# Attention and gated FFN in one fp32-exact kernel: values as one wide product a token tile, and the order at the seams

## The chip, the cores and the metric

One core of one Trainium2 chip. The metric is the device time of one execution in microseconds (us), the median of several. Engines: PE (TensorE, matmul), PEld (its weight loads), DVE (VectorE), ACT (ScalarE), POOL (GpSimd), SP (SyncE, which here only issues DMAs).

## The reference

`x` is 8 sequences of 1024 tokens with 512 features, fp32.

```
xn = layernorm(x)
heads: ql,kl,vl = xn @ local_qkv      full softmax attention
       qs,ks,vs = xn @ sparse_qkv     scores below the 102nd largest of a row masked, softmax
       xp = xn @ memory_proj; softmax(xp @ bank.T) @ bank; concat @ mem_out + b
       (xn @ pred_in + b) @ pred1 + b -> gelu -> @ pred2 + b
s = concat(4 heads of 128) @ warboss_w + b          # 512 x 512
g = silu(relu(xn @ w1 + b1) @ w2 + b2)              # 512 -> 2048 -> 512
out = x + s * g
```

## The kernel before

Every product is exact to fp32: each operand is split in a high part (rounded to fp32r, a reduced form of fp32 that PE takes) and a low part (the rest), and `product` (L72 to L76) issues three matmuls, high by high, high by low, low by high. So nearly every result of PE is read twice or more: a copy of the high part (a rounding copy by ACT) and a subtraction for the low part (by DVE or POOL).

**Stage 1** works over 16 halves of a sequence, 512 tokens each. It makes queries, keys, values and the memory and prediction heads, and writes them in split form to scratch arrays in DRAM. What PE does in a half is a list of jobs in the order of `JOBS` (L49; half 0 has `FIRST_JOBS`). mp and pi project for memory and prediction, ql, qs, kl, ks are queries and keys, ms the memory scores, p1a and p1b the first prediction layer (before gelu), wt the transposed memory weights, p2 the second layer, tr0 to tr3 transpose the next half's normalised tokens, mo is the memory output, v01 and v23 are the values of token tiles 0, 1 and 2, 3 (both value heads, 256 columns a tile). The jobs take six PSUM banks in turn: `PLACE` numbers them, `bank` is the place modulo 6, and a job waits until the bank of the job six places before it has been read (`bank_free`, semaphore `bank_read`, counted by ACT's last copy of each job). Where DVE reads the bank after ACT (mp, pi, wt) the next user waits for `lo_ready` too (`LOW_OF`).

All engines walk the same list. ACT (`scalar`, L564 on) copies each job out, does the gelu of p1a and p1b (L586, to SBUF) and of the values makes one copy (L620) and one rounded copy (L622). POOL (`gpsimd`, `left` L514 to L516) subtracts for the low parts of queries, keys, values and the FFN weights. DVE (`vector`, L798 on) makes the other low parts (`subtract`, L673), in gelu's case a rounding cast (L858) and a subtraction, and the softmax of the memory head. It also makes the layer norm of half n + 2 at the end of half n (`layer_norm_parts`, L675 to L715): statistics (L693, L696), then twelve steps of Newton's method for the inverse root on 128 x 4 elements (L699 to L707), then the application (L711). Halves 2 to 5 also split a quarter of the warboss weights there. Half 14 starts the search for the first slot on `early`, `scores` and `ranks`: ACT copies the scores (L649), DVE takes maxima (L766 on).

**Stage 2** works over 64 slots of 128 tokens. A slot has one row of scores for each attention head, PE's transposes of the probabilities, the outputs, the mixing product `mix`, and four chunks of the FFN: `f1` (hidden, `hid` or `o` from `xnT` and `w1`) and `f2` (`acc` from `w2` and `h`). DVE finds the 102nd largest score by rounds of MAX8 and MATCH_REPLACE8 over two half rows (L1561 to L1584), and between the rounds, at the round numbers `R_MAX` and `R_INVERSE`, takes the full row's maximum (`full_max`, L1529) and the inverse of its sum (`full_inverse`, L1535). The order of `f1`, `f2`, `transposes`, `head_scores` and `head_out` on PE is written out in `slot` (L1725 on; the last slot behind it). SP's DMA queue loads `w1`, `w2`, `tl` and the keys and values, in the order written in its `slot` (L1239 on). C is the number of a chunk, c its number within the sequence.

## Time and profile before

| | us |
|---|---|
| median of 3 runs | 2529.58 (2529.27 to 2530.76) |
| profiled execution | 2529.44, its span 2527.6 |
| PE busy | 2515.6 |
| DVE busy | 2291.1 |
| ACT busy | 1299.4 |
| POOL busy | 1151.8 |

The span runs from the first to the last instruction. Times of instructions are counted from the start of the span, so a row that starts at 246.78 lies in stage 1 (to about 485), one at 565.03 in slot 3 of stage 2. One half of stage 1 takes 29.14 us, one slot 31.83. The clock granted to TensorE was 1.00 of full speed throughout, the higher of its two levels.

### The profile page before, as it was taken

The numbers are of one execution on the slowest core, as the hardware profiler recorded it, in microseconds if no ns is written. First come the engines' busy times: TensorE is split into PE (matmuls) and PEld (weight loads), VectorE is DVE, ScalarE is ACT, GpSimd is POOL, SyncE is SP. The second block draws the span as 40 slices with busy tenths as digits, with TensorE's granted clock in tenths as the row PEclk, the third lists the DMA queues.
The fourth block names the chain that finished last, engine by engine and source line by source line (L and its number), as shares of the span: only waits on it lengthen the run. The fifth ranks groups of instructions, "written<-read, shape, count | busy, mean of one in ns | idle before, by whom it ended". The sixth has DMA issues, their size and how long they took to land.

```text
span 2527.6 us, 36088 instructions
## 1 busy us (share of the span) xinstructions
PE 2515.6 (100%) x12432; PEld 2120.0 (84%) x12432; DVE 2291.1 (91%) x5184; ACT 1299.4 (51%) x2128; POOL 1151.8 (46%) x975
## 2 busy tenths in 40 slices
PE   9999999999999999999999999999999999999999
PEld 8888888878888888888888888888888888888887
DVE  7566556999999999999999999999999999999995
ACT  5666666644444444444544444444444444444443
POOL 2544444533444444444444444444444444444444
PEclk9999999999999999999999999999999999999999
DMA  8888888964655565546554665466556654665443
GB/s 262 331 309 314 309 311 326 340 230 138 236 197 200 167 234 200 200 167 233 200 200 166 224 206 197 166 219 214 200 167 216 215 199 164 216 217 199 165 157 122
DMA packets 166149, 551.74 MB, mean 218 GB/s; under 512 B 17936, under 2 KB 32976, under 8 KB 157648
## 3 DMA queue, kind: packets, MB, share of 16 engines
q1 hardware_dynamic: 165680, 548.90, 61.9%
q8 instruction: 101, 1.65, 0.3%
q14 instruction: 80, 0.66, 0.1%
q10 hardware_dynamic: 288, 0.52, 0.1%
HBM read 415.15 MB, written 134.22 MB: 217 GB/s over the span
## 4 chain that ended last, share of the span: by engine, by line
PE 95%; DVE 4%; ACT 0%; issue 0%; POOL 0%; POOLq 0%; ACTq 0%
PE acc L74 9%; PE acc L76 9%; PE acc L75 9%; PE hid L76 9%; PE hid L74 9%; PE hid L75 9%; PE ps L74 5%; PE ps L76 5%; PE ps L75 5%; PE o L1709 4%; PE scores L1696 4%; PE o L1713 2%; PE scores L74 2%; PE scores L76 2%; PE scores L75 2%; PE o L75 2%
## 5 line engine op out<-in xcount | busy, mean ns | idle before, releaser
L1428 POOL TENSOR_TENSOR h_lo<-h,h_hi 128x512 fp32r<-128x512 f32 x254 | 336.0, 1323 | 719.7 <-ACT h_hi L1323 718.2
L1561 DVE MAX8 ranks<-early 128x8 f32<-128x512 f32 x819 | 564.7, 689 | 13.0
L1581 DVE MATCH_REPLACE8 early<-ranks,early 128x512 f32<-128x512 f32 x756 | 511.1, 676 | 0.0
L1322 ACT ACTIVATE h<-hid,small 128x512 f32<-128x512 f32 x255 | 175.7, 689 | 479.9 <-PE hid L76 479.8
L74 PE MATMUL acc<-w,h_hi 128*128 128x512 f32 x1016 | 408.0, 402 | 0.0
L76 PE MATMUL hid<-xnT,w 128*128 128x512 f32 x1020 | 397.5, 390 | 0.0
L74 PE MATMUL hid<-xnT,w 128*128 128x512 f32 x1020 | 397.0, 389 | 0.0
L75 PE MATMUL hid<-xnT,w 128*128 128x512 f32 x1020 | 396.8, 389 | 0.0
L76 PE MATMUL acc<-w,h_lo 128*128 128x512 f32 x1016 | 396.5, 390 | 0.0
L75 PE MATMUL acc<-w,h_hi 128*128 128x512 f32 x1016 | 396.5, 390 | 0.0
L1428 POOL TENSOR_TENSOR pT_s<-pT,pT_s 128x512 fp32r<-128x512 f32 x256 | 327.2, 1300 | 42.2 <-ACT pT_s L1337 42.2
L1565 DVE MAX8 ranks<-early 128x8 f32<-128x512 f32 x441 | 298.2, 676 | 0.0
L1584 DVE MATCH_REPLACE8 early<-ranks,early 128x512 f32<-128x512 f32 x378 | 255.6, 676 | 0.0
L76 PEld LDWEIGHTS acc<-w,h_lo 128*128 128x128 f32 x1016 | 190.7, 188 | 41.4
L74 PEld LDWEIGHTS hid<-xnT,w 128*128 128x128 f32 x1020 | 191.5, 188 | 40.3 <-DMA w<-ffn_scratch 0.4
L76 PEld LDWEIGHTS hid<-xnT,w 128*128 128x128 f32 x1020 | 191.5, 188 | 39.8
L75 PEld LDWEIGHTS hid<-xnT,w 128*128 128x128 f32 x1020 | 191.5, 188 | 39.6
L75 PEld LDWEIGHTS acc<-w,h_hi 128*128 128x128 f32 x1016 | 191.6, 189 | 33.6
L74 PEld LDWEIGHTS acc<-w,h_hi 128*128 128x128 f32 x1016 | 191.3, 188 | 33.7
L516 POOL TENSOR_TENSOR tiles_out<-tiles_out 128x512 fp32r<-128x512 f32 x64 | 95.1, 1495 | 227.3 <-ACT tiles_out L609 226.5
L1323 ACT ACTIVATE h_hi<-hid,small 128x512 fp32r<-128x512 f32 x253 | 172.6, 682 | 0.0
L1457 POOL TENSOR_TENSOR gate<-gate,mixed 128x512 f32<-128x512 f32 x60 | 77.8, 1297 | 186.1 <-DVE gate L1514 186.1
(237 smaller groups left out, 5170.2 us busy)
## 6 DMA issues: line engine op xcount, KB each, us to landing
w<-ffn_scratch SPq DMA_DIRECT2D x512, 512.0 KB, 4.1
xnT_scratch<-xnT SPq DMA_DIRECT2D x16, 2048.0 KB, 13.7
kv_scratch<-kv_out SPq DMA_DIRECT2D x32, 1024.0 KB, 6.1
tl<-tile_scratch SPq DMA_DIRECT2D x64, 512.0 KB, 4.0
tile_scratch<-tiles_out SPq DMA_DIRECT2D x15, 2048.0 KB, 8.5
xnT<-xnT_scratch SPq DMA_DIRECT2D x60, 512.0 KB, 7.1
ffn_scratch<-ffn SPq DMA_DIRECT2D x16, 1024.0 KB, 4.3
values<-kv_scratch SPq DMA_DIRECT2D x16, 1024.0 KB, 6.2
```

Source lines behind the costliest of these rows:

```text
L74: nc.tensor.matmul(out, w_hi, x_hi, start=first, stop=False)
L75: nc.tensor.matmul(out, w_hi, x_lo, start=False, stop=False)
L76: return nc.tensor.matmul(out, w_lo, x_hi, start=False, stop=last)
L1322: nc.scalar.activation(h32[:, c % 2, :], src[:, :], ACT.Relu, bias=bias)
L1323: nc.scalar.activation(h_of(C, c)[0], src[:, :], ACT.Relu, bias=bias).then_inc(h_h, 1)
L1428: return nc.gpsimd.tensor_tensor(out_, value, hi_.bitcast(F32), ALU.subtract).then_inc(ready, 1)
L1561: l_step = count(nc.vector.max(top_l[:, own], larger[:, :]))
L1565: s_step = count(nc.vector.max(top_s[:, own_s], smaller[:, :]))
L1581: l_step = count(nc.vector.match_replace(larger[:, :], top_l[:, own], larger[:, :], LOWEST))
L1584: s_step = count(nc.vector.match_replace(smaller[:, :], top_s[:, own_s], smaller[:, :], LOWEST))
L1696: last = nc.tensor.transpose(scores[:, j * P:(j + 1) * P], prob[own][:, j * P:(j + 1) * P], ident[:, :])
L1709: nc.tensor.matmul(o[:, :], units[unit][:, u, HI, c], pT_s[:, j, :, :, :], start=j == 0, stop=False)
```

## The change

1. The values are four jobs, v0 to v3, one a token tile. The high and low parts of the projection weights lie side by side in `wp_s`; a tile's high part is multiplied by both in one product of 512 columns (four of them, one for each quarter of the features), then its low part by the high weights in four of 256 columns. The three partial products then stand in two sums. ACT copies both to the two places of `kv_out` in one operation; POOL adds them, rounds the sum and subtracts, with a semaphore (`v_step`) between the steps.
2. Gelu: ACT applies it in place in PSUM, then makes the rounded copy; DVE subtracts each bank by itself, and its cast is gone. p1a and p1b are in `LOW_OF`.
3. The banks are shifted by four, since a half now has 20 jobs.
4. The layer norm of half 2, which DVE made whole at the end of half 0, is divided: statistics at the end of half 0, Newton's steps behind mp of half 1, the application behind pi.
5. At the seam of the stages: f1(0) and f1(1) wait for other banks; in slot 1 the two f2 stand before head_scores and before the second transposes, in slot 2 the f2 of chunk C stands before the wait for the transposes; in slot 3 the maximum of the full row and its inverse come one round earlier; SP issues w2(2) before tl(2) and w1(4) early.
6. In the last slot three f2 stand each one place earlier.

```diff
 JOBS = ["mp", "pi", "ql", "ms", "p1a", "p1b", "qs", "kl", "wt", "ks", "p2",
-        "tr0", "tr1", "tr2", "tr3", "mo", "v01", "v23"]
-FIRST_JOBS = ["mp", "pi", "ql", "ms", "p1a", "p1b", "qs", "kl", "ks", "v01", "wt", "tr0", "p2", "tr1", "mo", "tr2",
-              "tr3", "v23"]
+        "tr0", "tr1", "tr2", "tr3", "mo", "v0", "v1", "v2", "v3"]
+VALUES = ["v0", "v1", "v2", "v3"]
+FIRST_JOBS = ["mp", "pi", "ql", "ms", "p1a", "p1b", "qs", "kl", "ks", "v0", "v1", "wt", "tr0", "p2", "tr1", "mo",
+              "tr2", "tr3", "v2", "v3"]
 BANKS = 6
+BANK_SHIFT = 4
...
-    LOW_OF = {"mp": "xp", "pi": "pin", "wt": "wt"}
+    LO = ["xp", "pin", "first_gelu", "gelu", "wt"]
+    LOW_OF = {"mp": "xp", "pi": "pin", "p1a": "first_gelu", "p1b": "gelu", "wt": "wt"}
...
-        wp_hi = sb("wp_hi", [P, KT, 8 * P], F32R)
-        wp_lo = sb("wp_lo", [P, KT, 8 * P], F32R)
+        wp_s = sb("wp_s", [P, 2, KT, 8 * P], F32R)
+        wp_hi, wp_lo = wp_s[:, HI, :, :], wp_s[:, LOW, :, :]
...
-            return PLACE[n, name] % BANKS
+            return (PLACE[n, name] + BANK_SHIFT) % BANKS
...
-                        elif name in ("v01", "v23"):
-                            c = slice(2 * P * slot, 2 * P * (slot + 1))
-                            left(kv_out[:, 2:4, LOW, c], kv_out[:, 2:4, HI, c], kv_l)
+                        elif name in VALUES:
+                            c = slice(P * slot, P * (slot + 1))
+                            high, low = kv_out[:, 2:4, HI, c], kv_out[:, 2:4, LOW, c]
+                            done_steps = 2 * (HTILES * n + slot)
+                            nc.gpsimd.tensor_tensor(low.bitcast(F32), high.bitcast(F32), low.bitcast(F32), ALU.add)\
+                                .then_inc(v_step, 1)
+                            pool.wait_ge(v_step, done_steps + 1)
+                            nc.gpsimd.tensor_copy(high, low.bitcast(F32)).then_inc(v_step, 1)
+                            pool.wait_ge(v_step, done_steps + 2)
+                            left(low, high, kv_l)
                         else:
...
-                            last = nc.scalar.activation(gelu[:, c, :], src, ACT.Gelu, bias=b_p1[:, c:c + 1])
+                            nc.scalar.activation(src, src, ACT.Gelu, bias=b_p1[:, c:c + 1]).then_inc(gelu_step, 1)
+                            act.wait_ge(gelu_step, 2 * n + c + 1)
+                            last = nc.scalar.activation(gelu_hi[:, c, :], src, ACT.Copy)
...
-                        elif name in ("v01", "v23"):
-                            c = slice(2 * P * int(name == "v23"), 2 * P * int(name == "v23") + 2 * P)
-                            src = src.rearrange("p (t h n) -> p t h n", t=2, h=2)
-                            nc.scalar.activation(kv_out[:, 2:4, LOW, c].bitcast(F32)
-                                                 .rearrange("p h (t n) -> p t h n", n=P), src, ACT.Copy)
-                            last = nc.scalar.activation(kv_out[:, 2:4, HI, c]
-                                                        .rearrange("p h (t n) -> p t h n", n=P), src, ACT.Copy)
+                        elif name in VALUES:
+
+                            c = slice(P * int(name[1]), P * int(name[1]) + P)
+                            last = nc.scalar.activation(kv_out[:, 2:4, :, c].bitcast(F32),
+                                                        src.rearrange("p (s h n) -> p h s n", s=2, h=2), ACT.Copy)
...
+                    if n == 1:
+                        next(second)
                     if first(n):
                         dve.wait_ge(bkT_out, 1)
                         subtract(bkT_s[:, 1, :, :], bkT[:, :, :], bkT_s[:, 0, :, :]).then_inc(bkT_split, 1)
...
                                                    op0=ALU.add, op1=ALU.subtract).then_inc(lo_ready, 1)
                     if first(n):
                         low_weights(VL, 2)
+                    if n == 1:
+                        next(second, None)
                     if n in parts:
                         next(parts[n])
...
-                    dve.wait_ge(bank_read, done(n, "p1b"))
-                    nc.vector.tensor_copy(gelu_hi[:, :, :], gelu[:, :, :]).then_inc(ghi_ready, 1)
-                    dve.wait_ge(ghi_ready, n + 1)
-                    subtract(gelu_lo[:, :, :], gelu[:, :, :], gelu_hi[:, :, :]).then_inc(lo_ready, 1)
+                    for c, name in enumerate(("p1a", "p1b")):
+                        dve.wait_ge(bank_read, done(n, name))
+                        subtract(gelu_lo[:, c, :], ps[:, bank(n, name), :], gelu_hi[:, c, :]).then_inc(lo_ready, 1)
...
                         nc.vector.tensor_scalar(half_bias[:, :], half_bias[:, :], 0.5, None, ALU.mult)
-                    if n < LAST - 1:
+                    if first(n):
+                        next(second)
+                    elif n < LAST - 1:
...
-                        elif name in ("v01", "v23"):
+                        elif name in VALUES:
                             v = slice(VL * P, (VS + 1) * P)
                             if first(n):
                                 pe.wait_ge(w_split, 5)
-                            for tt in range(2):
-                                t = 2 * int(name == "v23") + tt
-                                c = slice(t * P, (t + 1) * P)
-                                for k in range(KT):
-                                    last = product(nc, dst[:, tt * 2 * P:(tt + 1) * 2 * P], xnT[:, hh, k, HI, c],
-                                                   xnT[:, hh, k, LOW, c], wp_hi[:, k, v], wp_lo[:, k, v],
-                                                   k == 0, k == KT - 1)
+                            c = slice(P * int(name[1]), P * int(name[1]) + P)
+                            for k in range(KT):
+                                nc.tensor.matmul(dst, xnT[:, hh, k, HI, c], wp_s[:, :, k, v], start=k == 0, stop=False)
+                            for k in range(KT):
+                                last = nc.tensor.matmul(dst[:, 0:2 * P], xnT[:, hh, k, LOW, c], wp_hi[:, k, v],
+                                                        start=False, stop=k == KT - 1)
...
+        FIRST_ROUNDS = {1: (1, 2), 3: (2, 3)}
...
-                sp.wait_ge(f1_done, C - W1_RING + 1)
+                sp.wait_ge(f1_done, 1 if C == 4 else C - W1_RING + 1)
...
+                    load_w2(2, 2)
                     load_tl(2, 2, 2)
-                    load_w2(2, 2)
+                    load_w1(4, 4)
                     load_w2(3, 3)
...
-                load_w1(C + 4, c + 4)
+                if m > 1:
+                    load_w1(C + 4, c + 4)
...
-                r_max, r_inverse = (1, 2) if m == 1 else (R_MAX[T % HTILES], R_INVERSE[T % HTILES])
+                r_max, r_inverse = FIRST_ROUNDS.get(m, (R_MAX[T % HTILES], R_INVERSE[T % HTILES]))
...
                 if C == 0:
-                    pe.wait_ge(shared.bank_read, PLACE[LAST, "wt"] + 1)
+                    pe.wait_ge(shared.bank_read, PLACE[LAST, "p2"] + 1)
                     pe.wait_ge(shared.w10_first, 16)
                     pe.wait_ge(shared.xnT_first, 16)
                 elif C == 1:
-                    pe.wait_ge(shared.bank_read, PLACE[LAST, "ks"] + 1)
+                    pe.wait_ge(shared.bank_read, PLACE[LAST, "mo"] + 1)
...
+                    if m == 2:
+                        f2(C, c, h)
                     pe.wait_ge(pT_h, 4 * g + 2)
                     pe.wait_ge(ps_ready, m)
                     transposes(2)
-                    f2(C, c, h)
+                    if m > 2:
+                        f2(C, c, h)
                     f1(C + 2, c + 2, h)
...
+                    if m == 1:
+                        f2(C, c, h)
                     pe.wait_ge(pT_h, 4 * g + 2)
                     head_scores(T % TL_RING, T_QL, U_KL, sl_done)
-                    f2(C, c, h)
+                    if m > 1:
+                        f2(C, c, h)
                     if not known_first(m, 2):
 
                         pe.wait_ge(mix_ready, m - 2)
                         mix(m - 2, (T - 2) % TL_RING)
                     f1(C + 2, c + 2, h)
+                    if m == 1:
+                        f2(C + 1, c + 1, h)
 
                     pe.wait_ge(pl_ready, m + 1)
                     transposes(0)
-                    f2(C + 1, c + 1, h)
+                    if m > 1:
+                        f2(C + 1, c + 1, h)
                     f1(C + 3, c + 3, h)
...
             f2(C, c, h, (0,))
             f1(C + 2, c + 2, h)
+            f2(C + 1, c + 1, h, (0,))
             pe.wait_ge(mix_ready, m - 2)
             head_out(g, U_VS)
             f1(C + 3, c + 3, h)
-            f2(C + 1, c + 1, h, (0,))
+            f2(C + 2, c + 2, h, (0,))
             pe.wait_ge(at_l, g + 1)
             mix(m - 2, (m - 2) % TL_RING)
-            for i in (2, 3):
-                f2(C + i, c + i, h, (0,))
+            f2(C + 3, c + 3, h, (0,))
             pe.wait_ge(mix_ready, m - 1)
```

On POOL, a half of stage 1 from the third on. Before, `kv_out` 128x2x256 are the low parts of the values:

```order
L516 TENSOR_TENSOR ffn<-ffn 128x2x512
L516 TENSOR_TENSOR kv_out<-kv_out 128x512 x2
L516 TENSOR_TENSOR tiles_out<-tiles_out 128x4x128 x2
L516 TENSOR_TENSOR kv_out<-kv_out 128x2x256 x2
L516 TENSOR_TENSOR tiles_out<-tiles_out 128x4x128 x2
```

With the change:

```order
L519 TENSOR_TENSOR ffn<-ffn 128x2x512
L519 TENSOR_TENSOR kv_out<-kv_out 128x512 x2
L519 TENSOR_TENSOR tiles_out<-tiles_out 128x4x128 x2
L535 TENSOR_TENSOR kv_out<-kv_out 128x2x128
L538 CAST kv_out<-kv_out 128x2x128
L519 TENSOR_TENSOR kv_out<-kv_out 128x2x128
```

The last three rows stand there four times, once for each of v0 to v3, where two operations stood.

On ACT, from the table load ahead of gelu. Before:

```order
L586 ACT_TABLE_LOAD
L586 ACTIVATE gelu<-ps,small 128x512 x2
L608 ACTIVATE tiles_out<-ps 128x4x128
L609 ACTIVATE tiles_out<-ps 128x4x128
L615 ACTIVATE kv_out<-ps 128x512
```

With the change:

```order
L596 ACT_TABLE_LOAD
L596 ACTIVATE ps<-ps,small 128x512
L598 ACTIVATE gelu_hi<-ps 128x512
L596 ACTIVATE ps<-ps,small 128x512
L598 ACTIVATE gelu_hi<-ps 128x512
L620 ACTIVATE tiles_out<-ps 128x4x128
```

Two copies now stand ahead of the copies of qs (`tiles_out`) and of all behind it.

On PE in slot 1, where `scores<-kl` is head_scores and `acc<-w2_0` is f2(0). Before:

```order
L74 MATMUL scores<-kl,tl1 128x512
L75 MATMUL scores<-kl,tl1 128x512
L76 MATMUL scores<-kl,tl1 128x512
L74 MATMUL acc<-w2_0,h_hi 128x512
L75 MATMUL acc<-w2_0,h_hi 128x512
L76 MATMUL acc<-w2_0,h_lo 128x512
```

With the change:

```order
L76 MATMUL acc<-w2_0,h_hi 128x512
L77 MATMUL acc<-w2_0,h_hi 128x512
L78 MATMUL acc<-w2_0,h_lo 128x512
L76 MATMUL scores<-kl,tl1 128x512
L77 MATMUL scores<-kl,tl1 128x512
L78 MATMUL scores<-kl,tl1 128x512
```

The twelve products of f2(0) moved ahead of the six of head_scores.

## Rows read from the trace of the kernel before

**Rows 1.** The page: busy time by engine, and the search's removal operation.

```profile
PE 2515.6 (100%) x12432; PEld 2120.0 (84%) x12432; DVE 2291.1 (91%) x5184; ACT 1299.4 (51%) x2128; POOL 1151.8 (46%) x975
...
L1581 DVE MATCH_REPLACE8 early<-ranks,early 128x512 f32<-128x512 f32 x756 | 511.1, 676 | 0.0
```

**Rows 2.** Windows: us; busy PE, PEld, DVE, ACT, POOL; PEclk, DMA share, GB/s.

```profile
161.10:190.24 29.14, 29.14 (x167) 25.46 (x166) 18.25 (x44) 19.19 (x38) 13.34 (x9) 1.00 0.82 307
493.90:565.00 71.10, 68.31 (x323) 56.17 (x321) 69.97 (x160) 32.97 (x51) 24.31 (x22) 1.00 0.71 254
```

**Rows 3.** Waits of PE: total us, times, longest.

```profile
PE scores L1696 <- ACT early L1372: 2.0, 1, 2.0
...
PE scores L1696 <- ACT pT_s L1337: 0.9, 1, 0.9
PE scores L74 <- ACT pT_s L1337: 0.7, 1, 0.7
...
PE o L1709 <- POOL pT_s L1428: 0.4, 1, 0.4
```

**Rows 4.** Timeline of PE, half 4: first and last of two runs of products.

```profile
134.10 0.39 PE L76 MATMUL ps<-xnT,wp_lo 128*128 128x512 f32 x1
...
139.54 0.39 PE L76 MATMUL ps<-xnT,wp_lo 128*128 128x512 f32 x1
...
154.97 0.28 PE L74 MATMUL ps<-wp_hi,xnT 128*128 128x256 f32 x1
...
160.60 0.28 PE L76 MATMUL ps<-wp_hi,xnT 128*128 128x256 f32 x1
```

**Rows 5.** Timelines of ACT, DVE and PE in half 0.

```profile
31.59 1.27 ACT L586 ACTIVATE gelu<-ps,small 128x512 f32<-128x512 f32 x2
...
38.22 0.69 DVE L673 TENSOR_TENSOR act_hi<-ps,act_hi 64x512 fp32r<-64x512 f32 x1 [1.35 <-ACT act_hi L577]
...
39.02 0.47 PE L74 MATMUL ps<-act_hi,sm_hi 128*128 128x512 f32 x1
```

**Rows 6.** Timeline of ACT, half 7.

```profile
239.69 0.69 ACT L605 ACTIVATE tiles_out<-ps,small 128x512 f32<-128x512 f32 x1 [0.27 <-PE ps L76]
```

**Rows 7.** Timelines of ACT, DVE and PE in half 14.

```profile
439.76 1.05 ACT L649 ACTIVATE early<-scores 128x1024 f32<-128x1024 f32 x1
...
440.83 1.77 DVE L766 TENSOR_TENSOR early<-early 128x512 f32<-128x512 f32 x1
...
446.67 0.48 PE L74 MATMUL ps<-act_hi,sm_hi 128*128 128x512 f32 x1
```

**Rows 8.** Timelines of POOL and PE in the last slot.

```profile
2508.79 1.30 POOL L1428 TENSOR_TENSOR xnT<-h,xnT 128x512 fp32r<-128x512 f32 x1
...
2510.15 0.49 PE L74 MATMUL acc<-w,xnT 128*128 128x512 f32 x1
```

**Rows 9.** Timelines of POOL, DVE and PE, end of half 7, start of half 8.

```profile
246.63 1.30 POOL L516 TENSOR_TENSOR kv_out<-kv_out 128x512 fp32r<-128x512 f32 x1 [1.19 <-ACT kv_out L622]
...
246.78 1.16 DVE L699 TENSOR_SCALAR small<-small 128x4 f32<-128x4 f32 x1
...
253.07 0.68 DVE L673 TENSOR_TENSOR act_lo<-ps,act_hi 128x512 fp32r<-128x512 f32 x1
...
256.33 0.22 PE L987 MATMUL ps<-bkT_s,act_hi 128*128 128x128 f32 x1
```

**Rows 10.** DVE's groups by line in stage 1: busy us, mean ns, idle before.

```profile
L705 DVE TENSOR_TENSOR small<-small 128x4 f32<-128x4 f32 x48 | 21.7, 452 | 1.6
...
L699 DVE TENSOR_SCALAR small<-small 128x4 f32<-128x4 f32 x16 | 15.1, 941 | 0.5
...
L701 DVE TENSOR_SCALAR small<-small 128x4 int32<-128x4 int32 x16 | 2.7, 172 | 0.6
```

**Rows 11.** Timeline of POOL in stage 2: operations of 256 columns.

```profile
507.93 0.74 POOL L1446 TENSOR_TENSOR pT<-pT 128x256 f32<-128x256 f32 x1 [0.80 <-ACT pT L1345]
508.73 0.40 POOL L1448 CAST at_hi<-pT 128x256 fp32r<-128x256 f32 x1
```

21 lines of the change are left out of this document (11 added, 10 removed).

## The prediction

> **What bounds the kernel now.** The page comes first. TensorE (PE) is busy for 2515.6 of 2527.6 us, VectorE (DVE) for 2291.1, ScalarE (ACT) for 1299.4, GpSimd (POOL) for 1151.8 [rows 1]. So the time is PE's own work plus some 12 us in which it stands. Next the table by stretches: in one half of stage 1, 161.10 to 190.24, PE is busy for 29.14 of 29.14 us at a granted clock of 1.00, while ACT works 19.19, DVE 18.25 and POOL 13.34 [rows 2]. PE is the only bound there, and the others have 10 us or more of room in sum, though not always where they need it. Then PE's waits: outside the start only a few are left, 2.0, 0.9 and 0.7 us at the border of the stages, for results of ACT, and 0.4 at the end [rows 3]. A change can win in two ways: fewer us of PE work, or those waits; it loses wherever something that PE waits for comes later than PE does.
>
> I count from the profiled execution, 2529.44 us. It is 0.14 below the median of the runs, 2529.58, so I add 0.14 at the end. What a measurement can tell from no change is about 0.2%, 5.1 us.
>
> **Values on PE.** In half 4 the last 48 products of 256 columns run from 154.97 to 160.60, 47 steps of 0.120 us. The products of 512 columns before them run from 134.10 to 139.54 in 24 steps of 0.2267 [rows 4]. A token tile had 12 of the narrow ones; it gets 4 wide and 4 narrow. Two narrow ones, 0.240, become one wide one, 0.2267: 0.0133 less, 16 times a half, 16 halves: **-3.4 us**. Read as a fixed cost and a cost by columns, both prices give 13 ns a product. The Trainium skill ("TensorE: Matmul & The Clock Gate", section "Wait — 56ns, not 53.3ns?") gives some 2.5 ns above the columns for each matmul in a warm stream; by it the 256 products fewer would bring only 0.6 us. Our rows show four to five times that, and the sum goes by them; if nothing at all were fixed, the gain would be 0, which is the upper end.
>
> **Gelu and startup.** ACT gets two copies a half (0.68 us each, by the neighbours in [rows 5]) and waits between gelu and copy; DVE's cast and its long subtraction become two subtractions of 512 from PSUM. In half 0 ACT is the bottleneck: after the gelus (1.27 for two, at 31.59) it works without a gap, then the DVE subtraction act_hi starts at 38.22 when ACT's act_hi has ended, 1.35 us after DVE was free, and PE's mo starts at 39.02 [rows 5]. The two copies, overlapped with their neighbours as ACT's operations are (starts 0.5 apart for durations of 0.6), and two short waits make some 1.2 us, all of it on this path: **+1.2**. Ends: 0.8 (a wait of PE before p2 of some 0.3 to 0.4 goes, because gelu_lo no longer is one long operation) to 1.6.
>
> **Half 1** gets the third layer norm's small operations before and between mp and pi. They come while POOL still works on half 0, whose values are now 12 operations. I take **+0.3**, ends 0 and 0.9 (one POOL operation of 0.74 each time for one of them).
>
> **The halves after.** Each has ACT 1.3 later from the gelus on. ACT itself waits 0.27 for PE at p2 before [rows 6], and its later results are wanted 0.3 to 0.7 after they come, as I read from their neighbours. So ACT may come some 0.3 late without cost, and its copies absorb the rest before tr0. I take **0**, ends 0 and +0.2 a half (2.4 over twelve).
>
> **Half 14**, where the first slot's search begins, has no room. ACT copies the scores at 439.76, DVE's first maximum follows at 440.83, and behind DVE's two passes over `early` act_hi and PE's mo come at 446.67 [rows 7]. That copy stands behind the gelus, so the whole chain moves by the two copies, 1.36, less the wait that PE shows now (0.15): +1.2, and with the waits **+1.4**; ends 0 (ACT's order lets DVE's subtractions catch up, since they save 0.5) and 1.8.
>
> **The border.** Waits of 0.7, 0.9 and 2.0 us are what can go [rows 3]. In slot 1 f2(C) now runs before head_scores and fills the first. But from 493.90 to 565.00 DVE is busy for 69.97 of 71.10 us [rows 2]: it is the bound behind the other two. head_scores starts 12 products of 0.2267, 2.7 us, later, less the wait of 0.7: the maximum that DVE takes of it comes 2.0 later, and everything behind it. Against that full_max moves one round forward in slot 3, and a round, two MAX8 and two MATCH_REPLACE8 of 676 ns each [rows 1], slightly overlapped, is 2.5 us. The two nearly cancel: 2.0 - 2.5 = -0.5 at slot 3's wait. I take **-0.3**, as w2(1), which f2(C+1) now wants 2.7 us earlier, may come a little late; ends -3.6 (all three go) and +1.0. On SP's queue w2(2) now passes tl(2), and w1(4) passes w2(3); neither is wanted within 4 us of its landing, so nothing.
>
> **The last slot.** The wait of 0.4 goes [rows 3], but POOL's h_lo, from 2508.79 to 2510.09, releases the next f2 at 2510.15 in both orders [rows 8]. **0**, ends 0 and -0.6.
>
> **Sum:** -3.4 + 1.2 + 0.3 + 0 + 1.4 - 0.3 + 0 = **-0.8**. 2529.44 - 0.8 + 0.14 = **2528.8 us**.
>
> **Rival B: POOL's twelve short operations block the layer norm, slower.** DVE's Newton steps are tiny operations that wait for POOL. In the half shown L699 starts at 246.78 and lasts 1.16, ending with POOL's 1.30 from 246.63 [rows 9]. Over stage 1 L699 takes 941 ns on average and L705 452, L701 of the same size 172 [rows 10]: a POOL operation under way blocks the DVE operation until its end. The Trainium skill ("SBUF — State Buffer", section "Who interferes with whom") says the same of a DVE operation that needs the port pair shared with GpSimd: who issues first keeps it for the whole instruction and the other fully blocks. The trace agrees: 941 against 172 ns. After the change POOL has, by the same forms in stage 2 (0.74, 0.40, and 0.73 for the subtraction) [rows 11], some 1.9 us for each of four value jobs, nearly without a gap, from about 246 to 254.4: over the whole Newton chain. If each of its 12 small operations gets in only between two of POOL's, the chain lasts 12 x 0.62 = 7.5 us instead of 4.5, from 247.5 (the subtraction of p1a and p1b and the mixing weights leave it 0.7 later) to about 254.9. The four applications and mp's low part (1.83 and 0.68, as now up to 253.75) end at 257.4. PE wants it at 256.33 [rows 9], 0.2 earlier with shorter values: up to 1.3 us a half; I take 0.85, as POOL's work is over by then and the last operations run free. Halves 1 to 13: 13 x 0.85 = 11. **2540 us.** It decides from the point where the chain gets longer by more than 1.7 us (2.4 of room, 0.7 used up by the later start). For it: 941 against 172 ns, in the half shown just while POOL was at work. Against: POOL waits for its own semaphores between its steps, and in each gap a DVE operation of 0.16 us may slip in, two or three one after the other; then 6 waits of 0.55 make 3.3, hardly over the room, and it costs next to nothing.
>
> **Rival C: the waits go and the new work hides, faster.** The startup and half 14 take less than I say because the DVE operations there no longer meet POOL (1.2 and 1.4 are then 0 to 0.4), and of the border's 3.6 us some 3 go: -3.4 - 3.0 - 0.6 = -7.0. **2522.6 us.** For it: each wait of [rows 3] is at a place which the change touches. Against: DVE nearly without a gap in [rows 2].
>
> **Rival D: ACT is late in every half.** If the 1.3 us of copies outrun ACT's room by 0.2 in twelve halves: 2528.8 + 2.4 = **2531.2**, not told from no change.
>
> **Rival E: the wide products do not save.** If the cadence is set by columns alone: 2528.8 + 3.4 = **2532.2**, also within 0.2%.
>
> **Chances.** My sum has 0.27, D 0.05, E 0.05: 0.37 for within 0.2% (2524.5 to 2534.6). B has 0.36, with mild forms of it counted in: slower. C has 0.27. The range leaves out the tails of B and C: from 2521 (C with a little more) to 2542 (B at 1 us a half). The likeliest case's own range is 2526 to 2533.
>
> **What would show it.** PE should show 12176 matmuls, 256 fewer, and about 2512 us of busy time with steps of 0.227 in the wide products. ACT's busy time should rise by some 22 us (32 copies of 0.68), DVE's fall by some 9 (32 of 0.68 in place of 16 of 0.68 and 16 of 1.2 or more, less what POOL blocks), POOL's rise by 16 x 5 = 80 (7.5 for 2.6). PE's waits should name act_hi in half 0 and in half 14 at about 1.3 each, and none in halves 2 to 13. B is right if PE waits for act_lo or for DVE's mp part at every ms, and L701 to L707 rise from 0.17 towards 0.6 us. C is right if the waits behind ACT at slots 1, 2 and 3 are gone. My forecast falls if PE stands anywhere in halves 2 to 13 for more than 0.3 us a half, or if the step of the wide products is not 0.227.

## The result, and the profile after

The changed kernel takes 2535.76 us (median of 13 runs, 2535.03 to 2536.47), the kernel before 2530.76 (13 runs, 2529.27 to 2531.46) in the same comparison: a ratio of 1.0021, 95% interval 1.0014 to 1.0028. It is slower by 5.0 us, 0.2%. The forecast was 2528.8 and no change; 2535.76 lies inside its range, but the kernel moved, and not by any one of the cases as they were told. The profiled execution took 2535.20, its span is 2533.4 against 2527.6. Executions of the kernel before come out near 2529.4 or near 2531.1 (e11 suggests why), so below, differences of medians under 1 us say little, and the profiles, one for each kernel, say more.

The page's busy times [rows 1]:

```profile
PE 2515.0 (99%) x12176; PEld 2105.5 (83%) x12176; DVE 2299.6 (91%) x5184; ACT 1316.4 (52%) x2160; POOL 1218.3 (48%) x1135
```

PE issues 256 matmuls less, and still the kernel is longer: PE stands more often. The signs of the forecast for the other engines were off too: ACT's busy time rose by 17.0 us (forecast 22), POOL's by 66.5 (80), and DVE's rose by 8.5 where a fall of 9 was forecast. PE's waits, total, times and longest [rows 3]:

```profile
PE ps L1003 <- DVE act_lo L683: 1.8, 5, 0.4
...
PE o L1727 <- DVE mixed L1541: 1.7, 1, 1.7
PE acc L76 <- DMA w<-ffn_scratch: 1.7, 1, 1.7
PE ps L76 <- ACT xnT L641: 1.2, 1, 1.2
PE ps L1017 <- DVE we L862: 1.0, 1, 1.0
PE o L76 <- DMA w<-ffn_scratch: 0.9, 1, 0.9
PE scores L1714 <- ACT early L1390: 0.8, 1, 0.8
PE acc L76 <- POOL h_lo L1446: 0.5, 1, 0.5
PE acc L76 <- POOL xnT L1446: 0.5, 1, 0.5
```

Where the 5.8 us of span are, by the starts of ms on PE (from half to half) and of slot 4's scores; "half n" below is the stretch from its ms to the next half's. The last column is the forecast, with the 0.2 a half that the shorter values were to give:

| stretch | before, us | after, us | difference | forecast |
|---|---|---|---|---|
| to ms of half 0 | 22.06 | 22.24 | +0.18 | 0 |
| from there to ms of half 1 | 30.22 | 31.28 | +1.06 | +1.0 |
| to ms of half 2 | 29.21 | 31.19 | +1.98 | +0.1 |
| to ms of half 6 | 116.56 | 118.32 | +1.76 | -0.9 |
| to ms of half 14 | 233.12 | 231.92 | -1.20 | -1.7 |
| to ms of half 15 | 32.03 | 31.72 | -0.31 | +1.2 |
| to the scores of slot 4 | 113.75 | 116.42 | +2.67 | -0.5 |
| the rest | 1950.6 | 1950.3 | -0.3 | 0 |

**Values.** PE's timeline of one tile, half 4:

```profile
159.15 1.07 PE L1038 MATMUL ps<-wp_s,xnT 128*128 128x512 f32 x4
160.05 0.64 PE L1040 MATMUL ps<-wp_s,xnT 128*128 128x256 f32 x4
160.53 0.86 PE L1038 MATMUL ps<-wp_s,xnT 128*128 128x512 f32 x3
```

From tile to tile it is 1.38 to 1.41 us, where twelve narrow products took 1.44 [rows 4]. A wide product takes 0.226 to 0.233 here. An undisturbed half is 28.98 us instead of 29.14, so the gain is 0.16 a half, 2.5 in all.

**Half 0.** Timelines of ACT, DVE and PE [rows 5]:

```profile
31.76 0.66 ACT L596 ACTIVATE ps<-ps,small 128x512 f32<-128x512 f32 x1
32.45 0.60 ACT L598 ACTIVATE gelu_hi<-ps 128x512 fp32r<-128x512 f32 x1
...
39.61 0.69 DVE L683 TENSOR_TENSOR act_hi<-ps,act_hi 64x512 fp32r<-64x512 f32 x1 [4.23 <-ACT act_hi L587]
...
40.41 0.47 PE L76 MATMUL ps<-act_hi,sm_hi 128*128 128x512 f32 x1 [1.19 <-ACT xnT L641]
```

mo starts at 40.41 instead of 39.02, of which 0.2 were there before half 0: the forecast's +1.2.

**Half 1.** Timelines of DVE and PE:

```profile
53.93 2.99 DVE L721 TENSOR_SCALAR early<-early,small 128x512 f32<-128x512 f32 x4
56.83 0.41 DVE L842 COPY mscore<-ps 128x256 f32<-128x256 f32 x1
...
62.43 0.63 PE L1017 MATMUL ps<-ident,we 128*128 128x128 f32 x4 [1.03 <-DVE we L862]
```

The layer norm's application stands ahead of the memory softmax's first copy, which starts 3.3 us after ms instead of 1.1 (before: 53.37, with ms at 52.28), and PE waits for the weights `we`.

**The ends of halves 1 to 5.** Timelines of DVE, POOL and PE, end of half 2 and start of half 3 [rows 9]:

```profile
105.09 0.65 DVE L709 TENSOR_SCALAR small<-small 128x4 f32<-128x4 f32 x1
105.77 0.67 DVE L711 TENSOR_SCALAR small<-small 128x4 int32<-128x4 int32 x1
106.47 0.17 DVE L713 TENSOR_SCALAR small<-small 128x4 f32<-128x4 f32 x1
...
110.47 2.48 DVE L721 TENSOR_SCALAR early<-early,small 128x512 f32<-128x512 f32 x4
112.87 0.68 DVE L683 TENSOR_TENSOR ww_lo<-ww_raw,ww_hi 128x512 fp32r<-128x512 f32 x1
113.47 0.68 DVE L683 TENSOR_TENSOR act_lo<-ps,act_hi 128x512 fp32r<-128x512 f32 x1
...
104.98 0.74 POOL L519 TENSOR_TENSOR kv_out<-kv_out 128x256 fp32r<-128x256 f32 x1
105.67 0.74 POOL L535 TENSOR_TENSOR kv_out<-kv_out 128x256 f32<-128x256 f32 x1
106.48 0.43 POOL L538 CAST kv_out<-kv_out 128x256 fp32r<-128x256 f32 x1
...
114.29 0.30 PE L1003 MATMUL ps<-bkT_s,act_hi 128*128 128x128 f32 x1 [0.39 <-DVE act_lo L683]
```

L709 ends with POOL's operation from 104.98 (105.74 and 105.72), L711 with the one from 105.67 (106.44 and 106.41), and then three small operations get through, while POOL rounds, before the next two are caught: six of the twelve are caught. The chain from L709 to the application takes 5.38 us; before it was 4.46. In halves 2 to 5 the subtraction of ww_lo, 0.68, stands behind it, and PE waits. act_lo, which PE waits for, ends 29.44 us after ms of its half instead of 27.17: the chain begins 0.8 later, is 0.9 longer, and the work behind it, beside POOL's last operations, takes 0.6 more. PE stands for 0.3 to 0.4 before each of the five ms, and halves 2 to 5 take 29.58 where the undisturbed ones take 28.98: 0.6 each.

**Half 14.** Timelines of DVE and POOL [rows 7]:

```profile
445.86 0.96 DVE L777 TENSOR_TENSOR early<-early 128x512 f32<-128x512 f32 x1 [1.20 <-ACT early L659]
446.75 0.68 DVE L778 TENSOR_TENSOR early<-early 128x512 f32<-128x512 f32 x1
...
446.84 2.84 POOL L519 TENSOR_TENSOR ffn<-ffn 128x1024 fp32r<-128x1024 f32 x1 [0.57 <-ACT ffn L675]
```

ACT's copy of the scores is later, as forecast, but the two passes, 1.77 and 2.88 us before, now take 0.96 and 0.68: they run ahead of POOL's long operation instead of beside it.

**The border.** Timelines of PE and DVE:

```profile
491.73 0.47 PE L76 MATMUL o<-xnT,w 128*128 128x512 f32 x1 [0.90 <-DMA w<-ffn_scratch]
...
495.23 0.50 PE L76 MATMUL acc<-w,h_hi 128*128 128x512 f32 x1 [0.53 <-POOL h_lo L1446]
...
504.00 0.47 PE L76 MATMUL acc<-w,h_hi 128*128 128x512 f32 x1 [1.68 <-DMA w<-ffn_scratch]
...
499.65 1.23 DVE L1547 TENSOR_REDUCE ranks<-scores 128x1 f32<-128x1024 f32 x1 [3.03 <-PE scores L78]
```

The waits of 0.7 and 0.9 of [rows 3] are gone, of the 2.0 before slot 3's transposes 0.8 is left, and waits of 0.9 (w1(1)), 0.5 (h_lo), 1.7 (w2(1)) and 1.7 (`mixed`) have come: 5.7 in all instead of 3.6. DVE, the bound of this stretch [rows 2], stands for 3.03 us before the full row's maximum, against 0.51 before.

### The profile page after: what moved, and what is told of

Its sections match the earlier page's. It is cut to its first block, busy times and chain, and to the rows that moved or that the text cites. A ratio compares the mean times of both kernels' runs of the same rounds, so it can differ in the third digit from the quotient of the medians.

```text
span 2533.4 us, 35773 instructions
## 1 busy us (share of the span) xinstructions
PE 2515.0 (99%) x12176; PEld 2105.5 (83%) x12176; DVE 2299.6 (91%) x5184; ACT 1316.4 (52%) x2160; POOL 1218.3 (48%) x1135
## 4 chain that ended last, share of the span: by engine, by line
PE 88%; DVE 7%; ACT 3%; POOL 1%; issue 1%; POOLq 0%; ACTq 0%; DVEq 0%
PE acc L76 9%; PE acc L78 9%; PE acc L77 9%; PE hid L78 9%; PE hid L76 9%; PE hid L77 9%; PE o L1727 4%; PE scores L1714 4%; PE ps L76 2%; PE ps L78 2%; PE ps L77 2%; PE o L1731 2%; PE scores L78 2%; PE scores L77 2%; PE scores L76 2%; PE o L76 2%
## 5 line engine op out<-in xcount | busy, mean ns | idle before, releaser
L519 POOL TENSOR_TENSOR tiles_out<-tiles_out 128x512 fp32r<-128x512 f32 x64 | 83.1, 1300 | 201.3 <-ACT tiles_out L621 198.1
```

## The experiments

Ratios are to the kernel before in the same comparison, 19 to 33 runs of it; where two kernels of different comparisons are set against each other, it is by these ratios. "The border" is the stretch from ms of half 15 to the scores of slot 4, 113.75 us before and 116.42 in the changed kernel.

**e1, values undone.** The changed kernel without its first and third point.

```diff
-        "tr0", "tr1", "tr2", "tr3", "mo", "v0", "v1", "v2", "v3"]
+        "tr0", "tr1", "tr2", "tr3", "mo", "v01", "v23"]
```

> The changed kernel with the values as before (v01, v23, products of 256 columns, two subtractions on POOL); gelu, layer norm, border and last slot as changed. Theory T (POOL's twelve short operations and their backlog cost the time): PE's waits of about 0.5 us before ms in halves 2 to 6 go, the wait for h_lo (0.7) at the border goes, and w1(1) and w2(1) land some 2 us earlier; the 2.2 us of shorter values are lost. From 2535.8: + 2.2 - 2.9 - 2 = about 2533. Rival O (the order written at the border costs the time whoever is late): the border still takes 2.7 us more than before and the total is about 2535 (+2.2 - 2.9).

2531.21 (10 runs) against 2529.90, ratio 1.0004 (0.9994 to 1.0013). The waits before ms in halves 2 to 6 are gone (29.14 us a half), the one in half 1 too, the one before mo of half 0 stays (1.7). The border takes 115.26, 1.5 more than before. But in this profile PE's clock fell there, behind the wait of 2.1 for w2(1):

```profile
500.13:503.40 3.27, 3.27 (x8) 2.62 (x9) 3.27 (x8) 1.50 (x3) 1.28 (x1) 0.50 0.98 397
```

The granted clock (third number from the end) is 0.50, and from 500.13 f2(1) takes 4.36 us to the transposes behind it, where the changed kernel takes 2.82 for the same twelve products. Without these 1.5 the border would take 113.7 (an estimate), as before: without POOL's new work the changed order costs nothing there, though it wins nothing either. So theory T holds for the waits before ms and for the border; only w2(1) did not land earlier.

**e2, border undone.**

```diff
-                    if m == 1:
-                        f2(C, c, h)
                     pe.wait_ge(pT_h, 4 * g + 2)
                     head_scores(T % TL_RING, T_QL, U_KL, sl_done)
-                    if m > 1:
-                        f2(C, c, h)
+                    f2(C, c, h)
```

(and the other lines of point 5 in the same way, but for the banks of f1(0) and f1(1))

> The changed kernel with the order of the border as before (f2 behind head_scores, full_max one round later in slot 3, w2(2) behind tl(2)), all else as changed. Theory T: the wait for w1(1), 1.06 us, stays, since that load waits for stores that POOL and ACT finish late; w2(1) is wanted 2.7 later and its 1.8 go; h_lo still waited for. Border about 1 us more than before instead of 2.7: total about 2534. Rival O: all 2.7 us go: total about 2533, with DVE's idle time of 3.0 before the full maximum of slot 1 back at 0.5.

2533.87 (10 runs), ratio 1.0015 (1.0005 to 1.0025), 1.5 below the changed kernel. In its profile the border takes 116.13, only 0.3 less. But the wait before slot 3's transposes is back at 2.4, and behind it PE's clock was at half for the eight transposes and four products: from the transposes at 568.46 to the next f1 at 573.77 it is 5.31 us, in the trace of before 3.69 (565.03 to 568.72). Without these 1.6 the border would take 114.5 (an estimate), 1.9 less than in the changed kernel and 0.8 more than before. That fits theory T (about 1 us more than before); the wait for w1(1) stays (0.9), as it says, and one of 0.9 for w2(1) is left.

**e3, layer norm undone.**

```diff
-                    if first(n):
-                        next(second)
-                    elif n < LAST - 1:
+                    if n < LAST - 1:
                         layer_norm(n + 2)
```

> The changed kernel with the third layer norm whole at the end of half 0, as before. Theory A (the application, placed between pi and the memory softmax of half 1, delays the softmax by 3.4 us, and PE waits for it): PE's wait of 1.2 before wt and the one of 0.3 before the values of half 1 go, half 1 is 1.5 shorter: 2534.3. Rival: at the end of half 0 the layer norm meets POOL's twelve operations, ms of half 1 waits for act_lo by 1.5 or more, and nothing is won: 2535.8.

2535.23 (10 runs), ratio 1.0021 (1.0012 to 1.0031): nothing won. The rival holds. The wait before wt is gone, and PE waits 1.5 for act_lo before ms of half 1 instead. By the table of starts half 0 takes 32.91 (31.28 in the changed kernel) and half 1 29.09 (31.19). With the values as changed and POOL at work to the end of half 0, the layer norm costs 1.6 to 2.1 us in either place.

**e4, gelu undone.**

```diff
-                            nc.scalar.activation(src, src, ACT.Gelu, bias=b_p1[:, c:c + 1]).then_inc(gelu_step, 1)
-                            act.wait_ge(gelu_step, 2 * n + c + 1)
-                            last = nc.scalar.activation(gelu_hi[:, c, :], src, ACT.Copy)
+                            last = nc.scalar.activation(gelu[:, c, :], src, ACT.Gelu, bias=b_p1[:, c:c + 1])
```

> The changed kernel with gelu as before (one activation to SBUF, DVE's cast and subtraction of 1024). Theory: ACT's two copies made mo of half 0 wait 1.35 us; that goes, the wait before p2 (0.4) comes back: -1. In the other halves DVE's subtraction of two SBUF operands meets POOL's longer work: it ends later, but PE wants it 1.5 us later: 0. Total 2534.8. Rival: the subtraction of 1024 is blocked by POOL in every half and the layer norm begins later still, so that the waits before ms grow from 0.5: total 2537 or more.

2531.07 (10 runs), ratio 1.0003 (0.9993 to 1.0012): 4.5 below the changed kernel, more than four times what was expected. Half 0 is 30.01, as expected, and half 1 30.89, 0.3 less. But halves 2 to 13 are all 28.99, the four with ww_lo too, though POOL does the same twelve operations and the chain takes 5.37. The waits before ms need both: ACT later by its two copies (so the tokens' low parts and with them the layer norm begin 0.8 later against PE: L709 20.4 us after ms, here 19.6) and the chain made longer by POOL. The forecast's rivals B and D were one mechanism, whose halves I had priced apart.

**e5, values alone**, on the kernel before.

> The kernel before with the values part alone (v0 to v3, wide products, twelve POOL operations); gelu, layer norm, border and last slot as before. Theory: halves 2 to 13 at 28.99 us without a wait (the runs without the new gelu had that), -0.15 each and 2.1 in all; the layer norm of half 2 at the end of half 0 meets POOL's backlog and ms of half 1 waits 1 to 1.5; at the border w1(1) and h_lo come late behind POOL, +2. Total 2529.9 - 2.1 + 1.3 + 2 = 2531. Rival: the border's loss needs the changed order too: 2529.

2534.80 (10 runs) against 2529.45, ratio 1.0020 (1.0011 to 1.0030). Halves 2 to 13 as expected (28.99). But ms of half 1 waits 3.6 us, not 1 to 1.5: Newton's twelve steps meet POOL's backlog of half 0 and take 5.6 us where they took 2.4, and the four applications take 2.86 where they took 1.92. And the wait costs more than itself. PE's windows during the wait, in the 5.5 us behind it, and after:

```profile
51.80:55.80 4.00, 0.39 (x2) 0.00 (x0) 3.96 (x7) 1.09 (x2) 1.78 (x2) 0.89 1.08 367
56.00:61.50 5.50, 5.50 (x17) 4.65 (x18) 1.61 (x4) 2.32 (x8) 0.00 (x0) 0.50 1.03 353
61.90:70.00 8.10, 8.10 (x39) 6.67 (x38) 3.83 (x9) 5.25 (x9) 3.38 (x2) 1.00 0.74 306
```

The granted clock is 0.50, the lower level of 1.2 GHz, for 17 matmuls; those of 512 columns take 0.427 where 0.227 is usual. Half 0 and half 1 together lost 6.3 us. In the changed kernel they lose 3.0, with the new gelu but the whole layer norm (e3) 2.6, and with the divided layer norm but the old gelu (e4) 1.5. The border takes 114.43 here, 0.7 more than before.

**e6, border alone**, on the kernel before.

> The kernel before with the changed order of the border alone. Theory (the order saves the waits of 0.7 and 2.0 but brings new ones, w2(1) wanted 2.7 us earlier than it can land, DVE idle 2.5 longer before the full maximum of slot 1): +0.5 to +1.5, with a wait for w2(1) of some 1.5 and the wait of slot 3 down from 2.0 to below 1. Total 2530.4 to 2531.4. Rival (the order is right and only the late POOL spoils it): 3 us less than before, 2527.

2530.20 (10 runs) against 2529.45, ratio 1.0003 (0.9993 to 1.0012); in the profile the border takes 114.14, +0.4, a little under what was expected. PE's waits there:

```profile
PE o L1712 <- DVE mixed L1526: 1.7, 1, 1.7
PE acc L74 <- DMA w<-ffn_scratch: 1.1, 1, 1.1
PE scores L1699 <- ACT early L1375: 0.9, 1, 0.9
```

Before they were 0.7, 0.9 and 2.0 [rows 3]: 3.6 are taken away and 3.7 put back. DVE stands 2.25 before the full row's maximum of slot 1, 1.7 more than before. The wait of 1.7 for `mixed` is new: `mixed` stands behind the same operations of DVE as before, the maximum among them in either order, so it comes no sooner; PE, let through sooner by the maximum, waits for it instead (e12).

**e7, wide values in halves 1 to 14 alone**, on the kernel before.

```diff
+LAST_JOBS = JOBS[:-4] + ["v01", "v23"]
...
-    return FIRST_JOBS if n == 0 else JOBS
+    return FIRST_JOBS if n == 0 else LAST_JOBS if n == LAST else JOBS
```

(`JOBS` has v0 to v3, `FIRST_JOBS` v01 and v23)

> The kernel before with the wide products in halves 1 to 14 alone; half 0 and half 15, where POOL has no room, keep v01 and v23, and nothing else is changed. Theory: 14 halves at -0.15, no new wait at the start, in half 1 or at the border: 2529.9 - 2.1 = 2527.8, faster than both kernels. Rival (POOL's longer work in half 14 is enough to make the border's stores and loads late, or the layer norm of half 3 waits): 2529.5 or more.

2528.29 (10 runs, 2526.45 to 2529.47) against 2529.45, ratio 0.9994 (0.9985 to 1.0004): below both kernels by the medians, clearly below the changed one, not told from the one before. Its profile has a span of 2524.6, and no new wait in stage 1 but 0.2 in half 14. At the border w2(1) is waited for by 1.5 in the old order too, and slot 3's wait falls from 2.0 to 0.7; the border takes 112.87.

**e8, ww_lo moved**, all else as changed.

```diff
-                    if n in MIXING_AT:
-                        k = MIXING_AT.index(n)
+                    if n - 1 in MIXING_AT:
+                        k = MIXING_AT.index(n - 1)
                         dve.wait_ge(ww_h, k + 1)
                         subtract(ww_lo[:, k, :], shared.ww_raw[:, k, :], ww_hi[:, k, :])
```

(the first from behind `layer_norm(n + 2)`, the second ahead of the low parts of tr0 to tr3)

> The changed kernel with the four subtractions for the low part of the warboss weights (0.69 us each) moved from behind the layer norm of halves 2 to 5 to the place before the token transposes' low parts of the next half, where DVE is idle for 2 us and more. Theory (the waits of 0.5 before ms in halves 3 to 6 are that subtraction in a chain that POOL has made longer; without it the chain just fits, as in halves 7 to 13): these four waits go, 2.4 us: 2535.5 - 2.4 = 2533, and the halves 3 to 6 take 29.0 instead of 29.6. Rival (the waits there come from something else in these halves, such as a late xn or ACT): they stay.

2532.76 (10 runs), ratio 1.0014 (1.0004 to 1.0023), 1.8 below the changed kernel, and 2.5 by the two spans. Half 2 takes 29.07 and halves 3 to 5 take 28.97, and of the five waits before ms one is left in that stretch (after half 1, which has no ww_lo and still catches up):

```profile
PE ps L1003 <- DVE act_lo L683: 0.3, 1, 0.3
```

This shows the 0.68 us of ww_lo to be what made the long chain too long, in four halves (with its place in DVE's order the chain itself came out at 4.85 in three of them). In the others it just fits: ahead of half 7 in the changed kernel act_lo ends at 231.86 and ms starts at 232.10.

**e9, the application behind the softmax.**

```diff
-                    if n == 1:
-                        next(second, None)
                     if n in parts:
...
                     if n in parts:
                         next(parts[n], None)
+                    if n == 1:
+                        next(second, None)
```

> The changed kernel with the application of the third layer norm (four operations, 3.0 us as they ran) moved behind the memory softmax of half 1, where the first slot of DVE time without a waiter is. Theory A (PE's waits of 1.2 before wt and 0.3 before the values of half 1 are this application standing ahead of the softmax's first copy): both go, half 1 takes some 29.5 instead of 31.2, and 2535.5 becomes 2534. Rival (the wait for the memory weights comes from Newton's steps or from ACT): it stays at 1.2.

2534.72 (10 runs), ratio 1.0019 (1.0010 to 1.0028). Half 1 is 28.99, even shorter than expected, but half 2 is 31.16: its waits are 0.4 before wt, 0.5 among the transposes and 0.7 before ms. The work was only pushed one half further: in half 2 everything from the tokens' low parts on stands 1.6 us later on DVE. Theory A held for its half and failed for the sum.

**e10, gelu alone**, on the kernel before.

> The kernel before with the gelu part alone. Theory: mo of half 0 waits for ACT as in the changed kernel (half 0 and 1 together 1.2 longer), all other halves 29.14, half 14 0.2 shorter since DVE's two passes over the first scores start after POOL's operation instead of beside it: 2529.5 + 1.0 = 2530.5. Rival (the two copies outrun ACT's room in every half): 2532 or more.

2530.44 (10 runs) against 2529.63, ratio 1.0003 (0.9994 to 1.0012). Half 0 is 31.59, +1.4; the others 29.12; half 14 is 0.2 shorter. As expected. The border takes 113.11.

**e11, last slot alone**, on the kernel before.

```diff
+            f2(C + 1, c + 1, h, (0,))
             pe.wait_ge(mix_ready, m - 2)
             head_out(g, U_VS)
             f1(C + 3, c + 3, h)
-            f2(C + 1, c + 1, h, (0,))
+            f2(C + 2, c + 2, h, (0,))
```

> The kernel before with the order of the last slot alone. Theory: the wait of 0.5 at head_out goes and one of 0.6 before the f2 that needs POOL's last h_lo takes its place: 0.0, 2529.5, and PE's last row no earlier. Rival: the 0.5 is won, 2529.0.

2529.72 (10 runs) against 2529.63, ratio 1.0000 (0.9991 to 1.0009). A wait of 0.5 for POOL's `xnT` before an f2 has taken the place of the one of 0.4, as expected. Its profile shows by chance why the kernel before has two groups of times. PE behind the wait of 2.0 in slot 3, where its code is that of before:

```profile
565.09 1.85 PE L1696 MATMUL scores<-ident,early 128*128 128x128 f32 x8 [1.96 <-ACT early L1372]
566.60 0.78 PE L74 MATMUL acc<-w,h_hi 128*128 128x512 f32 x1
567.17 0.63 PE L75 MATMUL acc<-w,h_hi 128*128 128x512 f32 x1
567.60 0.63 PE L76 MATMUL acc<-w,h_lo 128*128 128x512 f32 x1
```

The eight transposes took 1.85 instead of 1.09, and the products behind them 0.427 a step instead of 0.227: the clock fell after that wait, and it cost 1.6 us. In the profile of before it did not. That the second group of times is this drop is what the two profiles suggest; the unprofiled runs show no place.

**e12, the version of e7 with slot 3's maximum earlier and the last slot's order.**

```diff
-                r_max, r_inverse = (1, 2) if m == 1 else (R_MAX[T % HTILES], R_INVERSE[T % HTILES])
+                r_max, r_inverse = {1: (1, 2), 3: (2, 3)}.get(m, (R_MAX[T % HTILES], R_INVERSE[T % HTILES]))
```

> The kernel before with the wide products in halves 1 to 14 alone, the full row's maximum of slot 3 one round earlier, and the last slot's order; gelu, layer norm and the order of f2 at the border as before. Theory: the wait of 0.8 before slot 3's transposes that was left in the run with the wide products alone goes, as the maximum comes 2.5 us earlier; the last slot gives nothing: 0.8 less than that run, 2.5 to 3.5 below before, 2526.5. Rival (the freed time is spent at the next product that waits for DVE, the mixing of slot 3, as in the changed kernel's wait of 1.9): 2528.

2527.43 (11 runs, 2527.10 to 2527.85) against 2529.63 (33 runs), ratio 0.9991 (0.9982 to 1.0000): 2.2 us below before, at the edge of its interval, in one group of times instead of two. Its waits at the border:

```profile
PE o L1739 <- DVE mixed L1553: 1.7, 1, 1.7
PE acc L77 <- DMA w<-ffn_scratch: 0.9, 1, 0.9
PE scores L77 <- ACT pT_s L1367: 0.7, 1, 0.7
```

The rival is right: the 0.7 before the transposes went and 1.7 for `mixed` came. Timelines of DVE, slot 3, before and here:

```profile
570.11 0.67 DVE L1523 SCALAR_TENSOR_TENSOR mixed<-o,half_bias 128x512 f32<-128x512 f32 x1
...
569.01 0.67 DVE L1553 SCALAR_TENSOR_TENSOR mixed<-o,half_bias 128x512 f32<-128x512 f32 x1
```

Counted from ms of half 15 `mixed` starts at 106.9 before and at 107.2 here, and PE's product that needs it starts at 108.2 and at 107.9. So `mixed` was not made late by the moved maximum: it was the next thing on DVE that PE needed, and it did not move. Its profile is 1.4 longer than e7's and its median still lower, since none of its executions lies in the second group of times and five of e7's ten do.

**e13 and e14, the values of one half as before, all else as changed.**

```diff
+LAST_JOBS = JOBS[:-4] + ["v01", "v23"]
```

(e13; for e14 `FIRST_JOBS` has v01 and v23)

> The changed kernel with the values of half 15 alone as before (v01, v23, products of 256 columns, two long subtractions on POOL instead of twelve short operations); the other fifteen halves and all other parts as changed. Theory (POOL's backlog in the last half makes h_lo and, through the stores of tiles and values, the loads of w1(1) and w2(1) late): the wait for h_lo of 0.5 goes, those for w1(1) and w2(1), 0.9 and 1.7, lose 1 to 2 us together, the border takes 1.5 us less: 2534. Rival (the loads are late for another reason, so the border is the order's doing): the waits for both stay, 2535.5.

2534.60 (10 runs) against 2529.29, ratio 1.0019 (1.0009 to 1.0028). POOL's work ends 5.7 us earlier and the wait for h_lo is gone, but w2(1) is waited for longer:

```profile
PE acc L77 <- DMA w<-ffn_scratch: 2.8, 1, 2.8
PE o L1752 <- DVE mixed L1566: 1.7, 1, 1.7
PE o L77 <- DMA w<-ffn_scratch: 0.6, 1, 0.6
```

The border takes 0.5 less than in the changed kernel. The rival holds: f2(1) starts 37.4 us after ms of half 15, in the changed kernel 37.3, so what PE wins before w2(1) is lost at it.

> The changed kernel with the values of half 0 alone as before; all else as changed. Theory (the layer norm's application in half 1 took 3.0 us instead of 1.9 and Newton's steps came late because POOL still worked on half 0's values): 1 to 2 us of half 1 go, it takes some 29.5 to 30.2 instead of 31.2, total 2534. Rival (the place of the application alone delays the memory softmax, with POOL idle too): half 1 stays above 30.7, total 2535.5.

2532.84 (10 runs), ratio 1.0013 (1.0004 to 1.0023), 2.0 below the changed kernel, and 2.6 by the spans. Half 1 is 28.98 instead of 31.19. Timeline of DVE, half 1:

```profile
52.18 1.90 DVE L734 TENSOR_SCALAR early<-early,small 128x512 f32<-128x512 f32 x4
54.08 0.42 DVE L855 COPY mscore<-ps 128x256 f32<-128x256 f32 x1
```

The same four operations take 1.90 and not 2.99, Newton's steps 0.16 each, and PE waits for nothing. The place of the layer norm costs nothing; POOL's four value blocks of half 0 do.

## Why the prediction was wrong, point by point

- **Values on PE**, -3.4 forecast: -2.5 measured (0.16 a half). The mechanism held and the size was off by 0.9: the step of 0.2267 was read from the projections' products, and in the values' stream a wide product takes up to 0.233. Why it does is not shown.
- **Gelu and startup**, +1.2: held, +1.2 with its place and its wait (also e10).
- **Half 1**, +0.3: +2.1 (2.0 in the table, with the 0.16 of the values given back), the largest miss of one half. The step was "one POOL operation of 0.74 each time for one of them". It priced the small operations alone, and left out the four applications between pi and the softmax on DVE, which PE's `we` waits for. They come late by POOL's work of half 0, which ends at 52.03: with the old values in half 0 alone all of the loss is gone (e14), and with the applications in another place it only moves (e3, e9).
- **The halves after**, 0: PE waits before five ms, and four of the halves are 0.6 longer, 2.4 us. The step that failed is that ACT's copies are absorbed before tr0: the tokens' low parts and the layer norm behind them begin 0.8 later (e4). Rival B had the other half of the mechanism and mis-sized it: the chain grew by 0.9, not by 3.0, since half of its operations slip through, as the line against that rival said. With that, eight of its thirteen halves fit by 0.2 us. Of the five that do not, four carry ww_lo (e8), which I had left out of the chain's length, and they fail only with ACT's copies ahead (e4); the fifth follows half 1's loss.
- **Half 14**, +1.4: -0.15 (-0.31 with the shorter values). ACT was later as forecast, but I took the durations 1.77 and 2.88 as DVE's own; they held some 3 us of waiting for POOL, and one shift of 1.3 us freed them.
- **The border**, -0.3: +2.8. Two steps failed. "w2(1) may come a little late" was priced at 0.2: in the trace of before it is issued at 494.30 and lands 4.3 us later, at 498.6, for an f2 that started at 498.76. It had no margin, and the new order wants it 1.7 us earlier, not the 2.7 of the forecast, by which head_scores starts later (e6: a wait of 1.1; e13: 2.8). In the changed kernel it lands later too, 6.0 us after its issue. And the round by which full_max came earlier was taken as a gain of 2.5: slot 3's transposes wait 1.1 less, and at `mixed`, the next result of DVE that PE needs, which did not move with it, 1.7 came (e6, e12). That DVE would stand longer in slot 1 was right (forecast 2.0; 1.7 with the order alone, 2.5 in the changed kernel). What no step had is that these parts meet. By the profiles the border takes 113.75 before, 114.14 with the order alone (e6) and 114.43 with the values alone (e5); with the values and the gelu 114.5 (e2), with the order and the gelu 113.7 (e1), both without the drop of the clock; with the order and the values 115.73 (e4), and with all 116.42. So alone the order and the values cost 0.4 and 0.7, and together 2.0 to 2.7.
- **The last slot**, 0: held (e11).
- The forecast took seven terms as independent. e5 and e10 show +5.3 and +0.8 for two parts alone, e1 and e4 +1.3 and +1.2 for the change without one of these two: the parts do not add up, as at the border. That they share the room on DVE and POOL is how I read it.

Why w1(1) is late by 0.9 at the border can be followed on SP's queue. Its load waits until the store of the last FFN weights has landed, and that store stands behind others, of which the store of half 14's values waits for POOL. In us after ms of half 15:

| | values of half 14: store issued | FFN store landed | w1(1) issued | w1(1) landed | PE's wait |
|---|---|---|---|---|---|
| before | -6.86 | 17.97 | 17.99 | 23.38 | none |
| e1 (old values) | -6.87 | 18.74 | 18.76 | 23.78 | none |
| e4 (old gelu) | -4.80 | 19.18 | 19.19 | 24.06 | none |
| e13 (old values in half 15) | -3.92 | 19.75 | 19.76 | 24.75 | 0.6 |
| changed | -3.88 | 19.91 | 19.93 | 24.93 | 0.9 |

So it is half 14's values and the gelu together, and half 15's POOL work has little part in it (e13). No run moved that store alone, so this is read from the traces and not tested. What stays open: why w2(1) takes 6.0 us to land in the changed kernel where it took 4.3, and what the shift of the banks does, which no run took alone.

## What to carry to other kernels

When an operation is put into an engine's order, list what stands behind it there up to the next one that somebody waits for, and give each of those the delay; the moved layer norm was paid for by the softmax behind it, and the moved maximum took PE only as far as the next result of the same engine, which had not moved. A duration in a trace can be mostly waiting: before it enters a sum, compare it with the same form elsewhere. And an operand that is loaded just in time (landing at 498.6, used at 498.76) is a bound, not a detail, as soon as its user moves ahead. Last, look at the clock before two profiles are compared: in e1 and e2 some 1.5 us of the border were a drop of the clock behind one wait, and hid what the edit had won.

## What the runs showed of the hardware

- Small DVE operations against a row of POOL's short ones: L709 took 579 ns on average and L711 604, L713 170. Three get through while POOL rounds and the next two are caught by its subtraction and addition, so that the chain of twelve lost some 3.0 us beside eight short POOL operations, against 2.1 beside two long ones before (5.38 and 4.46 us for a chain that without POOL takes 2.4, as in half 1 of e14).
- PE's granted clock fell to 0.50 behind single waits of 2.0 us (e11), 2.1 (e1), 2.4 (e2) and 3.6 (e5), which cost 1.5 to 1.6 us of extra time in the first three and 2.9 in e5. In the profile of before the same wait of 2.0, in e3 one of 2.3 and in e13 one of 2.8 left it at 1.00. So such a wait can cost nearly twice its own length, in some executions and not in others.
- A pair of narrow products saved 10 ns when it became one wide product (0.16 us a half for 16 pairs). The Trainium skill ("TensorE: Matmul & The Clock Gate", section "Wait — 56ns, not 53.3ns?") gives some 2.5 ns a matmul above its columns; for this stream of pairs of weight load and product the trace shows four times that.
